# All eight adapters' A and B prepared once and written to memory, against one adapter prepared in every loop body

## The reference

```
w = weights[subject];  x1 = x + einsum('bct,bcd->bdt', x, w) + bias[subject][:, :, None]
H = einsum('btd,od->bto', x1, W)
xa = einsum('btd,brd->btr', x1, A[adapter])
delta = einsum('btr,bor->bto', xa, Bm[adapter]) * scalings[adapter]
out = x1 + H + delta
```

## Time and profile before

| | |
|---|---|
| time, median of 3 runs (lowest to highest) | 247.12 us (246.84 to 247.28) |
| the profiled execution's own time | 246.9 us |
| its span | 245.2 us |
| PE busy | 231.0 us (94% of the span) |
| DVE, ACT, POOL busy | 148.5, 109.9, 71.7 us |
| data moved | 36.56 MB, mean 149 GB/s |

### The profile page before, as it was taken

One profiled execution on the slowest core, in us unless ns is written; L12 is line 12 of the kernel. 1 busy time (PEld: TensorE's weight loads), 2 busy tenths in 40 slices (PEclk: granted clock), 3 DMA queues, 4 the chain that ended last, 5 costly groups with the idle time before them and its releaser, 6 DMA issues.

```text
span 245.2 us, 9843 instructions
## 1 busy us (share of the span) xinstructions
PE 231.0 (94%) x2917; PEld 188.8 (77%) x2919; DVE 148.5 (61%) x258; ACT 109.9 (45%) x191; POOL 71.7 (29%) x280
## 2 busy tenths in 40 slices
PE   1889999999999999999999999999999999999990
PEld 1667888888887888888888888888888888887750
DVE  6778856774457736775457736675457735345642
ACT  3265462552535353552535353562536343444621
POOL 3456501560046301560045501564134330000000
PEclk9999999999999999999999999999999999999998
DMA  6846564745465574745456563746455463641323
GB/s 143 264 137 144 172 179 130 208 118 166 135 178 141 153 192 110 215 121 178 125 164 152 150 196 107 210 114 192 127 153 161 136 195 111 199 124 45 88 54 77
DMA packets 23621, 36.56 MB, mean 149 GB/s; under 512 B 6066, under 2 KB 6066, under 8 KB 23602
## 3 DMA queue, kind: packets, MB, share of 16 engines
q1 hardware_dynamic: 16544, 26.36, 39.2%
q10 hardware_dynamic: 7058, 9.97, 14.1%
HBM read 19.53 MB, written 16.78 MB: 148 GB/s over the span
## 4 chain that ended last, share of the span: by engine, by line
PE 83%; DVE 6%; ACTq 2%; DMA 2%; issue 2%; ACT 2%; POOL 0%; SPq 0%; DVEq 0%; POOLq 0%
PE ps L851 66%; PE ps L820 13%; PE ps L796 3%; DMA x_ring<-in_x_dram 2%; ACTq L237 1%; DVE x_lo L529 1%; PE ps L755 1%; ACTq L675 1%; DVE o_ring L548 1%; DVE o_ring L544 1%; DVE m_lo L512 1%; ACT x_hi L640 1%; DVE x L521 1%; ACT m_f L662 0%; PE ps L790 0%
## 5 line engine op out<-in xcount | busy, mean ns | idle before, releaser
L851 PE MATMUL ps<-m_hi,x_hi 128*128 x248 | 99.4, 401 | 0.0
L851 PE MATMUL ps<-m_hi,x_lo 128*128 x248 | 96.8, 390 | 0.0
L851 PE MATMUL ps<-m_lo,x_hi 128*128 x248 | 96.6, 390 | 0.0
L529 DVE TENSOR_TENSOR x_lo<-x,x_hi 128x512 fp32r<-128x512 f32 x64 | 44.5, 696 | 62.7 <-ACT x_hi L640 62.6
L368 POOL COPY p_pair<-p_all 64x64 f32 x128 | 40.0, 313 | 124.5 <-DVE x L521 89.4
L640 ACT ACTIVATE x_hi<-x 128x512 fp32r<-128x512 f32 x64 | 40.4, 632 | 52.6 <-ACT o_ring L653 29.1
L653 ACT ACTIVATE o_ring<-ps 128x512 f32<-128x512 f32 x60 | 35.8, 596 | 56.7 <-PE ps L851 56.6
L851 PEld LDWEIGHTS ps<-m_hi,x_hi 128*128 128x128 f32 x248 | 46.6, 188 | 10.4 <-issue 0.2
L851 PEld LDWEIGHTS ps<-m_hi,x_lo 128*128 128x128 f32 x248 | 46.5, 188 | 10.1
L851 PEld LDWEIGHTS ps<-m_lo,x_hi 128*128 128x128 f32 x248 | 46.6, 188 | 9.1
L521 DVE TENSOR_TENSOR x<-ps,bias_pair 128x512 f32<-128x512 f32 x64 | 43.8, 686 | 9.1 <-PE ps L820 7.5
(11 more groups left out here) (101 smaller groups left out, 84.3 us busy)
## 6 DMA issues: line engine op xcount, KB each, us to landing
x_ring<-in_x_dram SPq DMA_DIRECT2D x124, 128.0 KB, 2.7
out_dram<-o_ring ACTq DMA_DIRECT2D x64, 128.0 KB, 2.6
out_dram<-o_ring SPq DMA_DIRECT2D x64, 128.0 KB, 2.3
a_f<-in_L_cond_A_dram SPq DMA_DIRECT2D x8, 128.0 KB
o_ring<-in_L_cond_W_dram SPq DMA_DIRECT2D x2, 256.0 KB, 4.3
o_ring<-in_L_cond_W_dram ACTq DMA_DIRECT2D x2, 256.0 KB, 5.6
x_ring<-in_x_dram ACTq DMA_DIRECT2D x4, 128.0 KB, 3.3
b_nat<-in_L_cond_Bm_dram ACTq DMA_DIRECT2D x1, 256.0 KB, 3.8
```

What stands on the lines that cost most here:

```text
L529: nc.vector.tensor_tensor(x1_lo[:, u % HELD], x1[:, u % 2], x1_hi[:, u % HELD], ALU.subtract).then_inc(x1_lo_ready, 1)
L851: mm = nc.tensor.matmul(ps[:, 2 + u % 2, :], part, m_tile(m, k, c), start=(c == 0 and part is hi and m is m_hi), stop=(c == TC - 1 and par ...
```

## The change

All eight adapters' A and B are prepared once, while pairs 0 to 5 run: SP loads all of A (128 rows), POOL scales all of B, PE turns it with four transposes (`turn_all`), ACT rounds and DVE splits both, and SP writes four results of 128 rows of 2 KB to memory (`store_parts`). From place 2 on, an adapter's parts are fetched from there by three transfers (`load_parts`): two copies of A's 16 high rows, two copies of its 16 low rows, two copies of B's 32 rows. PE waits for them with `parts_in`, ahead of the products. Places 0 and 1 stay as they were. Twelve pairs stand ahead of the loop instead of four, the loop has five bodies instead of six, and the products of place 2 go behind pairs 7 to 10 (behind 6 to 9 before); those of later places stay behind the same pairs. SP's program now has the same twelve pairs ahead of its loop.

```diff
-    HEAD = 4
+    HEAD = 12
-    BODIES = 6
+    BODIES = 5
...
+        a_dram = nc.dram_tensor("a_dram", (2, K, R, T), F32, kind="Internal").ap()
+        b_dram = nc.dram_tensor("b_dram", (K, 2, R, T), F32, kind="Internal").ap()
...
+            def store_parts():
+                sp.wait_ge(all_split, 2)
+                for part in range(2):
+                    sp.dma_start(a_dram[part].rearrange("k r t -> (k r) t"),
+                                 a_all[:, part].bitcast(F32)).then_inc(parts_out, 16)
+                    sp.dma_start(b_dram[:, part], b_all[:, part].bitcast(F32)).then_inc(parts_out, 16)
+            def load_parts(i):
+                k, = words(sp, regs[:1], order[0:1, ds(i, 1)], K - 1)
+                sp.wait_ge(parts_out, 64)
+                sp.wait_ge(m_summed, i * TC)
+                for part in range(2):
+                    sp.dma_start(a_parts[2 * R * part:2 * R * part + 2 * R, :].bitcast(F32),
+                                 a_dram[part, ds(k, 1)].to_broadcast([2, R, T])).then_inc(parts_in, 16)
+                sp.dma_start(b_parts[0:GR, :].bitcast(F32), b_dram[ds(k, 1)].rearrange("k q r t -> k (q r) t")
+                             .to_broadcast([2, 2 * R, T])).then_inc(parts_in, 16)
...
-                if n is not None and u == 0:
-                    load_a(n + 2)
+                if n is None and j == 0:
+                    sp.wait_ge(a_ready, 2)
+                    sp.dma_start(a_f[:], A.rearrange("k r t -> (k r) t")).then_inc(a_in, 16)
+                if n is None and j == 5:
+                    store_parts()
+                if n is None and j == 6:
+                    load_parts(2)
+                if n is not None and u == 4:
+                    load_parts(n + 3)
...
-                if n is not None and u == 7:
-                    dup_b(n + 2)
-                    pool.wait_ge(b_dupped, n + 3)
+                if n is None and j == 7:
+                    pool.wait_ge(b_turned, 2)
+                    nc.gpsimd.tensor_tensor(b_dup[:], b_nat[:].rearrange("p k (c r) -> p c k r", c=TC),
+                                            scal_all[:].unsqueeze(1).unsqueeze(3).to_broadcast([P, TC, K, R]),
+                                            ALU.mult).then_inc(b_all_scaled, 1)
...
-                if n is not None and u == HEAD + 1:
-                    a_split(n + 2)
-                    b_split(n + 2)
+                if n is None and j == 4:
+                    dve.wait_ge(all_rounded, 1)
+                    nc.vector.tensor_tensor(a_all[:, 1], a_f[:], a_all[:, 0], ALU.subtract).then_inc(all_split, 1)
+                    dve.wait_ge(all_rounded, 2)
+                    nc.vector.tensor_tensor(b_all[:, 1], b_turned_at(2), b_all[:, 0], ALU.subtract).then_inc(all_split, 1)
...
-                if n is not None and u == HEAD:
-                    a_round(n + 2)
-                    b_round(n + 2)
+                if n is None and j == 4:
+                    act.wait_ge(a_in, 48)
+                    nc.scalar.activation(a_all[:, 0], a_f[:], ACT.Copy).then_inc(all_rounded, 1)
+                    act.wait_ge(b_all_turned, 1)
+                    nc.scalar.activation(b_all[:, 0], b_turned_at(2), ACT.Copy).then_inc(all_rounded, 1)
...
-                if n is not None and u == HEAD:
-                    turn_b(n + 2)
+                if n is None and j == 4:
+                    turn_all()
...
-                    pe.wait_ge(a_ready, place_at + 1)
-                    pe.wait_ge(b_ready, place_at + 1)
+                    if isinstance(place_at, int) and place_at == 1:
+                        pe.wait_ge(a_ready, 2)
+                        pe.wait_ge(b_ready, 2)
+                    else:
+                        pe.wait_ge(parts_in, place_at * 48 - 48)
                     m_product(place_at * TC + chunk, chunk)
```

More of the change, by code:

```diff
@@ L51, in cond_residual_layers @@
     W_SUBJECT, W_PLACE = 0, 2
-    HEAD = 4
+    HEAD = 12
     BODY = 8
-    BODIES = 6
+    BODIES = 5
     TAIL = HEAD + BODY * BODIES
-    assert PAIRS == 64 and BODIES == K - 2 and TAIL % 4 == 0 and TAIL <= PAIRS - MIXED
+    assert PAIRS == 64 and BODIES == K - 3 and TAIL % 4 == 0 and TAIL <= PAIRS - MIXED
     with ExitStack() as ctx:
@@ L70, in cond_residual_layers @@
         b_parts = sb("b_parts", [P, T], F32R)
-        a_f = sb("a_f", [GR, T])
+        a_f = sb("a_f", [P, T])
         a_parts = sb("a_parts", [P, T], F32R)
-        b_nat = sb("b_nat", [P, K, TC * R])
         b_dup = sb("b_dup", [P, TC, P // R, R])
@@ L113, in cond_residual_layers @@
         order = sb("order", [1, K], I32)
+        with nc.sbuf_tensor("b_nat", [P, K, TC * R], F32) as b_nat:
+            pass
+        b_all = sb("b_all", [P, 2, T], F32R)
+        a_all = sb("a_all", [P, 2, T], F32R)
+        a_dram = nc.dram_tensor("a_dram", (2, K, R, T), F32, kind="Internal").ap()
+        b_dram = nc.dram_tensor("b_dram", (K, 2, R, T), F32, kind="Internal").ap()
         with nc.sbuf_tensor("wt", [P, TC, T], F32) as wt, nc.sbuf_tensor("x_ring", [P, XR, T], F32) as x_ring:
@@ L180, in cond_residual_layers @@
         a_ready = sem("a_ready")
+        b_all_scaled = sem("b_all_scaled")
+        b_all_turned = sem("b_all_turned")
+        all_rounded = sem("all_rounded")
+        all_split = sem("all_split")
+        parts_out = sem("parts_out")
+        parts_in = sem("parts_in")
         m_summed = sem("m_summed")
@@ L211, in pairs @@
             for j in range(head):
-                step(j, j, None)
+                step(j, j % BODY, None)
             with eng.Fori(0, BODIES) as n:
@@ L221, in tiles_of @@
             if n is not None:
-                return {6: [(n + 2, 0)], 7: [(n + 2, 1)], 0: [(n + 2, 2)], 1: [(n + 2, 3)]}.get(u, [])
-            return {1: [(1, 0), (1, 1)], 2: [(1, 2), (1, 3)]}.get(j, [])
+                return {6: [(n + 3, 0)], 7: [(n + 3, 1)], 0: [(n + 3, 2)], 1: [(n + 3, 3)]}.get(u, [])
+            return {1: [(1, 0), (1, 1)], 2: [(1, 2), (1, 3)],
+                    7: [(2, 0)], 8: [(2, 1)], 9: [(2, 2)], 10: [(2, 3)]}.get(j, [])
         def sums_of(j, u, n):
             if n is not None:
-                return {7: [(n + 2, 0)], 0: [(n + 2, 1)], 1: [(n + 2, 2)], 2: [(n + 2, 3)]}.get(u, [])
-            return {2: [(1, 0), (1, 1)], 3: [(1, 2), (1, 3)]}.get(j, [])
+                return {7: [(n + 3, 0)], 0: [(n + 3, 1)], 1: [(n + 3, 2)], 2: [(n + 3, 3)]}.get(u, [])
+            return {2: [(1, 0), (1, 1)], 3: [(1, 2), (1, 3)],
+                    8: [(2, 0)], 9: [(2, 1)], 10: [(2, 2)], 11: [(2, 3)]}.get(j, [])
         def n_of_mixed(j):
@@ L301, in step @@
                              o_ring[0:C, u % OR, :]).then_inc(even_out[u % OR], 16)
-            pairs(sp, step, 0)
+            pairs(sp, step)
             for slot in range(OR):
@@ L486, in a_split @@
                 dve.wait_ge(a_rounded, i + 1)
-                nc.vector.scalar_tensor_tensor(out=a_parts[0:GR, :], in0=a_parts[0:GR, :], scalar=neg[0:GR, 0:1], in1=a_f[:],
+                nc.vector.scalar_tensor_tensor(out=a_parts[0:GR, :], in0=a_parts[0:GR, :], scalar=neg[0:GR, 0:1], in1=a_f[0:GR, :],
                                                op0=ALU.mult, op1=ALU.add).then_inc(a_ready, 1)
@@ L615, in a_round @@
                 at_least(act, m_summed, i * TC)
-                nc.scalar.activation(a_parts[0:GR, :], a_f[:], ACT.Copy).then_inc(a_rounded, 1)
+                nc.scalar.activation(a_parts[0:GR, :], a_f[0:GR, :], ACT.Copy).then_inc(a_rounded, 1)
             def b_round(i):
@@ L747, in turn_b @@
                 pe.wait_ge(b_dupped, i + 1)
-                if not isinstance(i, int):
-                    pe.wait_ge(m_added, i * TC - 1 - TC)
-                elif i == 0:
+                if i == 0:
                     pe.wait_ge(scal_ready, 1)
@@ L757, in turn_b, with turn_all @@
                 mm.then_inc(b_turned, 1)
+            def turn_all():
+                pe.wait_ge(b_all_scaled, 1)
+                pe.wait_ge(m_added, TC - 1)
+                for c in range(TC):
+                    mm = nc.tensor.transpose(ps[:, b_bank(2), c * P:c * P + P],
+                                             b_dup[:, c].rearrange("p k r -> p (k r)"), ident[:])
+                mm.then_inc(b_all_turned, 1)
             pe.wait_ge(firsts_ready, 1)
@@ L895, in step @@
                     layer0(j + i, u + i)
-                if n is not None and u == HEAD:
-                    turn_b(n + 2)
-                if n is not None and u == HEAD + 2:
-                    pe.wait_ge(m_ready, n * TC + 2 * TC)
+                if n is None and j == 4:
+                    turn_all()
+                if n is not None and u == 6:
+                    pe.wait_ge(m_ready, n * TC + 3 * TC)
+                if n is None and j == 6:
+                    pe.wait_ge(m_ready, 2 * TC)
                 if n is None and j == TAIL + 1:
```

5 lines of the change are left out of this document (3 added, 2 removed).

## The result

The changed kernel takes **279.91 us**, the median of four runs (275.46 to 286.6); the kernel before took 247.09 us beside it. The ratio is 1.120 (95% interval 1.116 to 1.124). It rests on the two runs of 275.46 and 278.4 us; the other two show a lower mean granted clock and are left out of it, as such runs are in the ratios further on. The forecast of 259.5 us had the sign right, and the time lies above its range of 251 to 268.

A forecast was written before the change was run, and what follows sets the result against it. PE was taken to bound the kernel, covering other engines' savings. Transposes gone -2.5, head wait +5.9 and loop waits +9.0 made +12.4 us on the profiled 246.9, forecast 259.5 us at the median, slower; range 251 to 268.

The forecast's parts named there:

- Rival 2: Loads of parts spread like x transfers, landing 2.7 us after an issue: 246.9 or 245.8 us, same or faster; chance 0.13.
- rival 3: Loads pay their fixed parts one behind the other, 14.6 us; a body waits 8.1 us, total about 297; chance 0.03.
- Rival 1: The three loads have engines of their own, landing 7.1 us after first issue: +4.1, 251.2 us, still slower; chance 0.16.
- the head up to layer 1 of pair 8: Ahead of the loop, PE waits behind pair 7 for place 2's parts: +5.9 us, from 3.6 to 9.3.
- The clock is no term.: Whole kernel: no cost from the clock, as the granted clock stood at 1.00 with PE working 0.88 of the first 6 us.
- five bodies: In the loop, PE waits for the loads behind the pair with u = 6: 1.8 us a body, 9.0 in five.
- the transposes gone: On PE, five sets of four transposes are removed at 0.50 us a set: -2.5 us.
- the high end: Loads landing 9.5 us after first issue and slow stores: -2.5 + 9.3 + 15 = +21.8, 268.9 us, taken as 268.
- 43.3 (42.2 ..., 45.5 ...): In the head, the time in us when the stores of parts have landed: 43.3, or 42.2 fast and 45.5 slow.
- 8.3 us after the first issue: Landing of the last row when all three loads share two engines: 3.15 us fixed plus 5.14 of data.

The follow-up runs named there:

- experiment 10: experiment 1's kernel with only its two loads' source pattern altered, so that two copies are the outermost dimension again: 285.37 us.
- experiment 1: Changed kernel with parts fetched by two loads, outermost dimension 32 or 64 rows, instead of three loads; B's parts twice in memory: 250.95 us, ratio 1.013.
- Experiment 12: experiment 1's kernel, place 2's products two and two behind pairs 9 and 10, ScalarE issuing its loads (pair 7) and two stores (pair 4): 248.09 us.
- experiment 3: Changed kernel with each loop load issued one step earlier, at pair 3 of a body instead of pair 4: 267.66 us.
- experiment 4: Changed kernel with 46 matmuls of zeros behind layer 1 of pair 7, keeping PE busy in the head's wait: 277.22 us.
- experiment 5: experiment 1's kernel, place 2's products two and two behind pairs 9 and 10, SP taking its loads at pair 7's step: 249.58 us, ratio 1.008.

## Why the prediction was wrong

The mechanism was right: three loads share two engines, land later than PE wants them, and PE stands once in the head and once in each body. Rival 2 fell by the landing times, and rival 3 too: the 9 us of a body are far from 14.6, and experiment 10's two loads land no sooner than the changed kernel's three. Rival 1 falls too: it wanted 7.1 us, and no landing came under 8.6. Loads on engines of their own, issued 1.0 us apart with 1.3 us of data each, would overlap at a share of 0.25, and the 2.3 us from 48.60 stay at 0.13. The semaphore that the loads raise agrees: in the last body its late updates come in pairs, at 202.80 and 202.85, 204.14 and 204.33, and 207.37 and 207.74 us, two for each load and one load behind the other, where a load of experiment 1 has sixteen.

The Trainium skill's rule (page "DMA: Bandwidth & Descriptors", section "Why a DMA increments its semaphore by 16 and not by 1") that the slowest dimension sets the number of engines agrees with experiments 1 and 10: as many bytes to the same place land in 3.5 or in 8.7 to 11.2 us. The Trainium skill's 2.0 us and bytes over 436 GB/s (same page, section "Anatomy of one DMA", written for another issuing engine) would hold roughly for experiment 1's last load (an estimate of 2.3 us, 2.73 measured) and not for two engines.

What was mis-sized or left out, on profiled executions:

| term | predicted | measured |
|---|---|---|
| the head up to layer 1 of pair 8 | +5.9 us | +11.5 |
| the clock | "no term" | +2.2 and +1.7 |
| five bodies | +9.0 | +14.3 |
| the transposes gone (measured: with all else) | -2.5 | -1.1 |
| sum | +12.4 | +28.6 |

The sum missed by 16.2 us: 5.6 in the head, 5.3 in the bodies, 3.9 at the clock and 1.4 at the transposes. Against the high end (+21.8: 9.3, 15 and -2.5) the head is 2.2 over, the bodies are 0.7 under, the transposes 1.4 short, and the clock adds 3.9: it is the largest part of what lies outside the range.

1. **The step that failed in kind is "The clock is no term."** It rested on a clock of 1.00 in the first 6 us of the earlier trace rows, where PE had just been busy for 0.88 us in pieces. A forecast that puts 5.9 us of idling into a chain of matmuls had to ask what the clock does behind it; the rows before have no such stretch in the loop, so it should have been bounded and was not. In the profiled execution it cost 3.9 us; the three others are 3 to 11 us longer, at lower mean clocks.
2. **The head.** The stores landed at 45.56, the slow end of "43.3 (42.2 ..., 45.5 ...)", and the loads took 10.94 us where 8.3 was taken and 9.5 was the high end. That the x transfers issued behind them lengthened it was not tried; in the semaphore's updates the third load lands 4.6 us behind the second here and 3.2 to 3.7 us behind it in the bodies, whose x transfers are issued later. The two delays add, since the loads wait for the stores.
3. **The body.** "8.3 us after the first issue" was 8.6 to 9.7, so the waits came to 10.5 us instead of 9.0. The larger share of the error is what the forecast left out: a body that waits costs more than the wait's length, here 0.75 us, most of it the longer product and the issuing behind it.
4. **The transposes.** Experiment 12 shows -0.34 a body, -1.7 in five, instead of -2.5.

The range ended at 268 because the head's bound was too low and the clock had none.

## What to carry to other kernels

Before a load with copies is moved into a loop, look at its outermost dimension: two copies of 32 rows and 32 rows of two copies are as many bytes, and here 26 us apart in the fastest runs and 34 at the median (experiments 1 and 10). Price a new wait of a busy TensorE as its length, plus some 0.75 us to get going, plus a layer at the lower clock whenever the idling may bring one. When work is moved onto a queue in the head of a program, list what that queue already issues there: in five repairs the wait went from the parts to x, to the rounding of x and back.

## What the runs showed of the hardware

- Short idling can bring the lower clock, and does not always. Behind waits of 2.42, 2.42, 1.98 and 1.72 us in the changed kernel's loop layer 1 ran in 3.0 us, behind the fifth, of 2.00 us, in 4.60; in experiment 3 a wait of 1.29 us was enough, in experiment 4 one of 1.97 us was and one of 2.61 us was not, nor in experiment 5 one of 2.54 us; in experiment 10 all six were followed by a slow layer 1. What decides between them no run here shows.
- A load of two copies moved 49 GB/s at a DMA share of 0.13, two engines at 24.5 GB/s each, and three such loads from one queue used the same two. Where other transfers ran beside them the loads' 256 KB took up to 11.2 us from the first issue.
- With B's stores spread over all engines 1.5 MB landed 8.3 us after the first store's issue, where 1 MB with B's in blocks had taken 8.8.
